# Self attention in a perceiver block: value products ahead of the next scores, quantization first in its slot, V and output projection in other slots

## What is computed

```python
x = x + xattn(layernorm(x), ctx, mask)    # 4 heads of 128, one shared K/V, 1601 context rows, rotary
x = x + attn(layernorm(x), WQ, WK, WV, WO)  # 16 heads of 32, causal, over the 64 rows
x = x + ffn(layernorm(x), W_fc, ln, W_proj) # gelu, layernorm, both weights quantized to -1, 0, 1
```

```python
Q, K, V = (heads(WQ), heads(WK), heads(WV))
score = jnp.einsum('bhqd,bhkd->bhqk', Q, K) / jnp.sqrt(jnp.asarray(D_K, x.dtype))
score = score + mask
...
out = jnp.einsum('bhqk,bhkd->bhqd', score, V)
return out.transpose(0, 2, 1, 3).reshape(B, S, E) @ WO
```

## Time and profile before

| | |
|---|---|
| runs | 1119.79, 1122.02, 1123.69 us (median 1122.02) |
| profiled execution | 1122.38 us, span of its trace 1120.2 us |
| PE busy | 956.8 us (85%) |
| DVE busy | 688.4 us (61%) |
| ACT busy | 453.0 us (40%) |
| POOL busy | 441.0 us (39%) |
| DMA | 95.11 MB, mean 85 GB/s |
| mean granted clock of PE | 0.969 |

### The profile page before, as it was taken

How to read it: one execution, slowest core, us unless ns; L and a number is a source line. 1 busy time by engine, 2 the same in 40 slices (tenths; PEclk the granted TensorE clock), 3 DMA queues, 4 the chain that set the end, 5 groups by cost and what they waited for, 6 DMA issues and landing times.

```text
span 1120.2 us, 22904 instructions
## 1 busy us (share of the span) xinstructions
PE 956.8 (85%) x7466; PEld 809.4 (72%) x7466; DVE 688.4 (61%) x1352; ACT 453.0 (40%) x972; POOL 441.0 (39%) x572
## 2 busy tenths in 40 slices
PE   0898879888788888779798988889869999999996
PEld 0787757676676767668688887778647888888885
DVE  3587666766766767764545554655556665565554
ACT  2565445554455545444323232434363322322321
POOL 1354444444444444410212111111016767667663
PEclk9999999999999999979799998999879999999999
DMA  5532233221223222411534443334331111101101
GB/s 167 156 92 55 71 89 95 89 60 59 84 83 92 72 80 73 158 38 40 170 116 112 114 136 95 107 108 108 107 118 38 58 34 52 57 29 57 57 19 50
DMA packets 96769, 95.11 MB, mean 85 GB/s; under 512 B 41634, under 2 KB 58099, under 8 KB 96371
## 3 DMA queue, kind: packets, MB, share of 16 engines
q1 hardware_dynamic: 96016, 93.19, 28.3%
q10 hardware_dynamic: 578, 0.13, 0.1%
q0 software_dynamic: 32, 0.02, 0.0%
HBM read 76.45 MB, written 12.66 MB: 80 GB/s over the span
## 4 chain that ended last, share of the span: by engine, by line
PE 66%; DVE 15%; issue 10%; ACT 3%; DVEq 2%; ACTq 1%; POOL 1%; DMA 1%; SPq 0%; POOLq 0%
PE bank L244 52%; PE bank L219 9%; PE bank L240 4%; DVE f L233 3%; DVE f L507 2%; DVE f L930 2%; DVEq L74 1%; ACT f L230 1%; ACTq L74 1%; ACT f L412 1%; PE bank L529 1%; DVE f L974 1%; DVE f L470 1%; DMA f<-in_L_attn_WO_dram 1%; DVE f L641 1%
## 5 line engine op out<-in xcount | busy, mean ns | idle before, releaser
L244 PE MATMUL bank<-f,f 128*128 128x512 f32 (+3 forms) x5544 | 762.0, 312 | 62.4 <-issue 24.5
L244 PEld LDWEIGHTS bank<-f,f 128*128 128x128 f32 (+2 forms) x5544 | 596.5, 173 | 165.9 <-issue 67.6
L233 DVE TENSOR_TENSOR f<-bank,f 128x512 fp32r<-128x512 f32 x291 | 194.4, 686 | 129.9 <-ACT f L230 127.9
L219 PE MATMUL bank<-f,f 128*128 128x128 f32 x1152 | 170.3, 282 | 62.9 <-DVE f L619 28.7
L230 ACT ACTIVATE f<-bank 128x512 fp32r<-128x512 f32 x291 | 167.1, 593 | 110.3 <-PE bank L219 105.5
L219 PEld LDWEIGHTS bank<-f,f 128*128 128x128 f32 x1152 | 136.8, 145 | 90.1 <-DVE f L619 29.8
L936 POOL TENSOR_TENSOR f<-f,f 128x512 f32<-128x512 f32 x32 | 33.4, 1043 | 219.0 <-DVE f L933 219.0
L1153 ACT ACTIVATE f<-bank 128x512 f32<-128x512 f32 x64 | 38.3, 599 | 175.5 <-PE bank L244 175.5
L1176 POOL TENSOR_TENSOR f<-f,f 128x512 f32<-128x512 f32 x62 | 79.7, 1285 | 67.4 <-DVE f L1172 67.4
L468 POOL TENSOR_TENSOR f<-f,f 128x512 f32<-128x512 f32 x32 | 41.9, 1310 | 156.6 <-ACTq L74 135.2
L1178 POOL TENSOR_TENSOR f<-f,f 128x512 f32<-128x512 f32 x62 | 80.5, 1299 | 4.9
(11 more groups left out here) (88 smaller groups left out, 819.0 us busy)
## 6 DMA issues: line engine op xcount, KB each, us to landing
f<-in_ctx_dram SPq DMA_DIRECT2D x71, 256.0 KB, 2.8
f<-x_scratch SPq DMA_DIRECT2D x64, 256.0 KB, 3.0
f<-in_x_dram SPq DMA_DIRECT2D x32, 256.0 KB, 3.0
x_scratch<-f SPq DMA_DIRECT2D x32, 256.0 KB, 2.0
f<-in_L_ffn_W_fc_dram SPq DMA_DIRECT2D x32, 256.0 KB, 3.0
f<-in_L_ffn_W_proj_dram SPq DMA_DIRECT2D x32, 256.0 KB, 3.2
f<-in_ktab_dram SPq DMA_DIRECT2D x71, 64.0 KB, 2.0
f<-f SPq DMA_DIRECT2D x64, 64.0 KB, 2.4
```

Source lines behind the costliest of these rows:

```text
L219: f = lambda e, i=i, a=a: e.transpose(dst[:, i, :], a, ident[0:rows, 0:rows])
L233: return maybe("dve", lambda e: e.tensor_tensor(lo, src, hi.bitcast(F32), ALU.subtract), sem(name + "_lo"), waits, when)
L244: f = lambda e, i=i, a=a, b=b: e.matmul(dst, a, b, start=(first and i == 0), stop=(last and i == n - 1), skip_group_check=check)
```

## The change

Value products move from order 4 to order 0.5 of their slot, ahead of the scores of the next item (order 1). The transposes of the result move one slot ahead, the output projection from slot s + 6, order 4.45, to s + 5, order 5.6. V of an item moves from slot s - 1 to s + 2, for all pairs but the first. The input transposes and the Q/K chunks move one slot back, from the third pair on. The second half of the exponential gets order 4.6 instead of 4.0. Quantization and absolute sums get order 0.3, the first in their slot, and `w_T(n)` stands on its own at order 4.5 of the same slot.

```diff
--- before.py
+++ after.py
@@ -1028,8 +1028,6 @@
 
         if n == 32:
             w_gamma()
-        else:
-            w_T(n - 1)
         m = (n - 32) // 16
         w = wq_[:, n % 2, :]
         tq = op("dve", lambda e: e.tensor_scalar(w, wn[:, n % 4, :], gam[:, m:m + 1], -1.0,
@@ -1066,19 +1064,19 @@
         at(o - 1, 0, lambda i=i: ln_load(i))
         at(o, 3.4, lambda i=i: ln_stats(i))
         at(o + (1 if u > 1 else 3), 4.3, lambda i=i: ln_apply(i))
-        at(B2 + 8 * u - 11 + v if u > 1 else T0 + 10 * u, 5, lambda i=i: s2_T(i))
-        at(s - 1 if u else T0 + 10 + v, 4.4, lambda i=i: s2_v(i))
+        at(B2 + 8 * u - 10 + v if u > 1 else T0 + 10 * u, 5, lambda i=i: s2_T(i))
+        at(s + 2 if u else T0 + 10 + v, 4.4, lambda i=i: s2_v(i))
         at(s, 1, lambda i=i: s2_scores(i))
         for b in range(2):
-            at(s + 1, 3.0 + b, lambda i=i, b=b: s2_exp(i, b))
+            at(s + 1, 3.0 + 1.6 * b, lambda i=i, b=b: s2_exp(i, b))
             at(s + 2 + b, 2.7, lambda i=i, b=b: s2_PT(i, b))
-        at(s + 4, 4, lambda i=i: s2_PV(i))
+        at(s + 4, 0.5, lambda i=i: s2_PV(i))
         at(s + 4, 0, lambda i=i: res_load(i))
-        at(s + 5, 5.5, lambda i=i: s2_ET(i))
-        at(s + 6 if i else s + 8, 4.45, lambda i=i: s2_O(i))
+        at(s + 4, 5.5, lambda i=i: s2_ET(i))
+        at(s + 5 if i else s + 7, 5.6, lambda i=i: s2_O(i))
     for u in range(ni // 2):
         for c in range(8):
-            at(B2 + 8 * u - 9 + c if u > 1 else T0 + 2 + c + 10 * u, 4.1 if u > 1 else 0.7,
+            at(B2 + 8 * u - 8 + c if u > 1 else T0 + 2 + c + 10 * u, 4.1 if u > 1 else 0.7,
                lambda u=u, c=c: s2_qk(u, 1 - c // 4, c % 4))
     at(T0, 4.5, s2_start)
     at(T0 - 9, 0, s2_x)
@@ -1101,11 +1099,11 @@
         if n < 4:
             at(B2 - 1, 0.5, lambda n=n: w_load(n))
         if n < 32:
-            at(s + 3, 3.9, lambda n=n: w_abs(n))
+            at(s + 3, 0.3, lambda n=n: w_abs(n))
         else:
-            at(s + 3, 4.5, lambda n=n: w_quant(n))
+            at(s + 3, 0.3, lambda n=n: w_quant(n))
+            at(s + 3, 4.5, lambda n=n: w_T(n))
     B3 = B2 + 4 * ni
-    at(B3 - 1, 9, lambda: w_T(63))
```

## The result

The changed kernel takes 1172.12 us (median of 4 runs, 1168.17 to 1172.78), the kernel before 1121.83 us (4 runs): ratio 1.0441, 95% interval 1.0412 to 1.0471. The forecast was 1175 us. The profiled executions took 1172.78 and 1122.38 us, a difference of 50.4 us against +52.4 in the sum.

The account below looks back on a forecast made before the run. TensorE was taken to bound the self attention, so only its waits and clock could change; 39.3 + 26.4 + 2 - 20.6 - 3 + 6.3 + 2 = +52.4 us on 1122.38 us gave 1175 us, range 1150 to 1198.

Parts of the forecast that it names:

- V's path and its wait: Pairs 1 to 6: value products wait for V's 5.9 us path of copy and DMAs, 39.3 us in all.
- The step on the landing: End of V's path: the last of four DMAs lands 3.0 us after its issue begins.
- The waits for L974 and L233: First two stretches: existing waits go, 20.6 us; new small waits of 16.3 us at full clock, some 2 us staying.
- Quantization opens its slot: Quantization no longer stands behind the score masks; part of taking all 20.6 us idle in the first two stretches as gone.
- the slower products give VectorE time: Behind clock falls, only some 2 us of the 16.3 us of small waits for VectorE stay.
- The clock: A fall in each of twelve items that wait for V, 2.2 us each, 26.4 us in all.
- the fall that was to go: Kernel before, at 681.9 us: the half-clock stretch of 6.4 us after two short waits disappears, winning 3 us.
- Rival (a): V is waited for but the clock holds, small waits come in full: +38.3 us, 1161 us; chance 0.25.
- The last pair and the hand-over: Pair 7, without Q/K products, and the feed-forward hand-over: waits of 21.6 us against 15.3 us, +6.3 us.
- ScalarE passes the snapshot ... TensorE starts: Hand-over: weight copies wait for V's DMAs, TensorE starts after VectorE's first copy, 8.8 us after V, 7.3 us idle.
- the start: Items 0 and 1: reordered value products and output projection exchange work for work, costed at nothing, +-3 us.
- rival (b): V has landed when the value products come: -7 us, 1115 us, or 1099 us with small waits covered; chance 0.07.

Follow-up runs that it names:

- the filled kernel: The change with ten unread 128x512 products put directly ahead of the value products of items 2 to 14: 1166.62 us, ratio 1.0393.
- The two kernels on the hand-over: The change with V in s + 1, plus item 15's value products behind the first feed-forward product (1104.20 us) or its second probability transposes one slot earlier (1102.86 us).
- the two kernels with V late: Kernel before with V alone moved to s + 2: 1125.34 us; the change with the output projection back in s + 6, V left in s + 2: 1126.99 us.

## Why the prediction was right, point by point

**V's path and its wait: right, 28.6 us instead of 39.3.** The path measured 5.4 us against 5.9 taken. The step on the landing put 3.0 us for it; here the value products started 2.6 us after the fourth issue. The Trainium skill's fit ("DMA: Bandwidth & Descriptors", section "Anatomy of one DMA") gives an estimate of 2.15 us and so a path of 5.0, as far off on the other side. Without quantization the waits were 3.4 and 2.5 us where 4.0 and 3.2 were forecast, both 0.6 to 0.7 less, of which the shorter path is 0.5. With quantization the first item of a pair waits 2.9 us (3.4 forecast), but in two of the three second items only 0.7 us, which the profile puts down to no DMA. In the timeline of one (what counts is the idle time in brackets):

```profile
733.41 0.40 PE L1048 MATMUL bank<-f,f 128*128 128x128 bf16 x4 [1.02 <-DVE f L1036]
733.65 0.61 PE L219 MATMUL bank<-f,f 128*128 128x128 f32 x4
734.95 2.48 PE L244 MATMUL bank<-f,f 64*64 64x33 f32 x123 [0.70 <-issue]
...
739.41 2.91 PE L244 MATMUL bank<-f,f 32*64 32x64 f32 x15 [1.98 <-issue]
```

TensorE waits 1.0 us for the quantization between V, which ended at 729.68, and the value products, and that time covers the path as well as work would. The value products start 5.3 us after V (5.2 us in the other item), so the 0.7 us is counted as V's, though no row names the DMA. The six items of pairs 1 to 3 sum to 3.40 + 3.37 + 3.37 + 2.49 + 2.48 + 0.63 = 15.7 us (the last of them behind 1.5 us of waiting for the gamma), those of pairs 4 to 6 to 2.89 + 2.86 + 2.89 + 0.70 + 0.65 + 2.86 = 12.9 us.

**The waits for L974 and L233: right; those for the quantization: wrong.** "Quantization opens its slot" was taken to end these waits but for some 2 us. In pairs 4 to 6 eight of them remain, 1.0 to 1.75 us, 9.9 us together. The step said that the slower products give VectorE time. They do, and the filled kernel, without falls, shows how much: ahead of the output projection it waits 1.5 to 2.2 us an item for the quantization. In the same items of the change that wait is 1.0 and 1.2 us shorter behind the two falls of 6.8 us (1.17 and 0.99 us, against 2.13 and 2.15), 0.5 us shorter behind two of the falls of 3.4 us (1.21 and 1.24, against 1.75), and as long behind the third (1.51) and where there is no fall (1.75). So a fall takes away about half of such a wait or less. Two of the eight waits, 1.0 us each, stand between V and the value products, where the forecast had none. The 8 us above the forecast made up for most of the 10.7 us by which V's wait was taken too large: the idle time of the first two stretches was forecast at 39.3 + 2 = 41.3 us and is 17.1 + 25.9 = 43.0.

**The clock: right in kind, too large.** A fall was priced at 2.2 us an item and expected in twelve. One pair shows 35.40 us of busy time against 32.30, 1.55 us an item. The price leaned on a fall of 6.4 us and on the whole of products and scores at the lower level. Here four falls are that long, six last 3.4 us, and one item has none: 47.8 us together, where twelve of 6.4 us are 77. Per microsecond at the lower level the price was right: 2.2 / 6.4 is 0.34, and 15.3 us (below) over 47.8 is 0.32. What was too large is the length. Over the first two stretches the busy time grew by 219.7 - 207.4 = 12.3 us, or 15.3 with the 3 us of the fall that was to go, where 26.4 was forecast. Rival (a), that the clock holds, is refuted by a clock of 0.89 and 0.91; "near 0.85" was too low, and a pair took 41.5 us, not 43 to 45. One reading of the earlier trace rows was off too: a mean of 0.86 is 0.28 us at half clock and not 0.1, so that fall lasted from 681.7 to 688.5, 6.8 us, and the one at 794 (mean 0.68, so 0.64 us at half clock, from 794.36) began 0.85 us into the idle stretch that starts at 793.51.

**The last pair and the hand-over: the size nearly right, one step missed.** Item 14 waited 4.33 us (4.8 forecast) and the quantization's transposes 3.94 and 4.39 (4.3 and 5.15). The hand-over idled 10.8 us where 7.3 was forecast. The step that failed is "ScalarE passes the snapshot ... TensorE starts" with VectorE's first copy: with the value products ahead of the feed-forward product, they wait for the copy L949, which ScalarE has behind both weight copies, 3.7 us. The two kernels on the hand-over show this. In sum the third stretch idled 23.6 us, 21.6 forecast.

**The sum.** Forecast: idle +27.0 (39.3 + 2 - 20.6 + 6.3), clock +25.4 (26.4 + 2 - 3). Measured: idle +30.7, clock +16.3, and 3.4 us behind the hand-over, for which the forecast had no term; the start, for which +-3 us were left, came to about nothing. The total is closer than its terms deserve, and that is luck: the clock was put 9 us too high, idle time and the stretch behind the hand-over 7 us too low.

**What the prediction didn't say.** It named only what covers the path after the change. That the kernel before has 7.5 us of cover for a V just as late, and that the missing 3 us of the output projection decide, came from the two kernels with V late. Nor did it see that V's early place leaves the quantization waited for longer: the change with V back is 0.5% slower than the kernel before, where rival (b), V landed in time, had 1115 us.

## What to carry to other kernels

When a producer with a path over several engines and DMAs is moved nearer to its consumer, add up the consumer engine's own work between them, item by item, and look whether the same change also takes some of it away: here 3 us of cover decided over 45 us. Work without a consumer nearby can be cover for a queue that is behind: V one slot earlier gave 5.5% against the changed kernel and 1.1% against the kernel before, though that it gains by this cover is read from the waits and not shown by a run of its own. At a hand-over that waits for a snapshot, look at each queue for what of the old stage still stands behind the waiting instruction.

## What the runs showed of the hardware

The granted clock fell at different points around waits of the same kind: 2.25 us after the end of an idle stretch of 2.49 us (609.6 us against 607.39), 1.2 us before the end of one of 3.37 us (626.7 against 627.93), and in the kernel before 0.85 us into a gap. In the waits for V it stayed down 3.4 us six times and 6.8 us four times, and one of the twelve items had no fall. In the kernel before the fall at 681.7 us lasted 6.8 us. With the gaps filled by wide products it stayed at full level from 570 to 829 us through the same order of small products. An idle stretch of 2.5 to 3.4 us thus cost another 1.55 us of slower products. Not all of that is won back when the falls go: in the filled kernel 7.1 us of waits for VectorE came back.
